# A graph attention kernel on one core: a third staged group of weights, and the order of ScalarE's first steps

## What is computed

```python
def _L0(h, adj, a):                      # slope 0.01, values h
    src = h @ a1; dst = h @ a2
    e = src[:, None] + dst[None, :]
    e = where(e > 0, e, 0.01 * e)
    e = where(adj > 0, e, NEG_INF)
    return softmax(e, axis=1) @ h
def _L1(h, adj, W, a):                   # slope 0.2, values Wh, elu behind
    Wh = h @ W
    e = leaky_relu((Wh @ a1)[:, None] + (Wh @ a2)[None, :], 0.2)
    return elu(softmax(where(adj > 0, e, NEG_INF), axis=1) @ Wh)
x = _layernorm(x + _L0(x, adj, L0_gnn_a))
x = _layernorm(x + _L1(x, adj, L1_gnn_W, L1_gnn_a))
```

## Time and profile before

| | |
|---|---|
| median of 3 runs | 438.73 us (438.42 to 439.5) |
| the profiled execution | 442.47 us, its span 440.6 us |
| busy: PE, VectorE, ScalarE, POOL | 408.1, 382.2, 382.9, 254.4 us |
| chain of work that ended last | PE 74%, VectorE 12%, issue 5%, DMA 5% |
| mean granted TensorE clock | 0.988 |

### The profile page before, as it was taken

One profiled execution on the slowest core, in us unless ns is written; L12 is line 12 of the kernel. 1 busy time (PEld: TensorE's weight loads), 2 busy tenths in 40 slices (PEclk: granted clock), 3 DMA queues, 4 the chain that ended last, 5 costly groups with the idle time before them and its releaser, 6 DMA issues.

```text
span 440.6 us, 11844 instructions
## 1 busy us (share of the span) xinstructions
PE 408.1 (93%) x4484; PEld 399.5 (91%) x4484; DVE 382.2 (87%) x682; ACT 382.9 (87%) x590; POOL 254.4 (58%) x293
## 2 busy tenths in 40 slices
PE   1599999999999999999999998999999999999980
PEld 1488889999999999999998898999999999999980
DVE  3789898899898998999889988679999999999963
ACT  3879796988969799779998989999999999999930
POOL 5523174572756637388294125659696969696831
PEclk9999999999999999999999999999999999999995
DMA  5999889989998999979510000000000000000000
GB/s 115 96 107 104 74 72 90 87 77 87 84 95 72 90 85 77 98 63 95 56 75 13 2 25 2 1 25 1 27 1 25 0 25 0 24 1 26 1 25 16
DMA packets 22766, 22.48 MB, mean 51 GB/s; under 512 B 1344, under 2 KB 22464, under 8 KB 22720
## 3 DMA queue, kind: packets, MB, share of 16 engines
q0 software_dynamic: 17424, 16.78, 44.3%
q1 hardware_dynamic: 4208, 4.05, 2.8%
q10 hardware_dynamic: 1088, 1.05, 0.7%
HBM read 69.30 MB, written 2.10 MB: 162 GB/s over the span
## 4 chain that ended last, share of the span: by engine, by line
PE 74%; DVE 12%; issue 5%; DMA 5%; POOL 1%; ACT 1%; DVEq 0%; POOLq 0%
PE acc L1222 66%; PE tb L1146 5%; DMA enc<-in_adj 3%; DVE neg L831 3%; DVE pos L842 2%; DMA mask_t<-in_x 1%; PE srcb L1156 1%; DVE mask_t L757 1%; DVE mask_t L814 1%; DVE split L814 1%; DVE wmov L820 1%; DVE scr L857 1%; ACT neg L670 1%; PE pg L1190 1%; DVE enc L814 1%
## 5 line engine op out<-in xcount | busy, mean ns | idle before, releaser
L1222 PE MATMUL acc<-wmov,pos 128*128 128x195 bf16 x2016 | 358.8, 249 | 5.0 <-DVE pos L842 3.8
L670 ACT ACTIVATE neg<-srcb,dcol 128x512 int8<-128x512 f32 x512 | 357.9, 988 | 3.4 <-PE acc L1222 3.2
L1222 PE MATMUL acc<-wmov,neg 128*128 128x195 bf16 x2016 | 358.9, 249 | 0.0
L1222 PEld LDWEIGHTS acc<-wmov,pos 128*128 128x128 fp8e4 x2016 | 199.1, 99 | 9.1 <-DVE pos L842 7.1
L1222 PEld LDWEIGHTS acc<-wmov,neg 128*128 128x128 fp8e4 x2016 | 198.1, 98 | 2.4 <-issue 1.3
L842 DVE TENSOR_TENSOR pos<-neg,mask_t 128x1024 uint16<-128x1024 uint16 x128 | 103.5, 809 | 14.1 <-PE acc L1222 0.9
L831 DVE TENSOR_TENSOR neg<-neg,mask_t 128x1024 uint16<-128x1024 uint16 x128 | 103.7, 811 | 11.6 <-ACT neg L670 9.1
L490 POOL DMA_DIRECT2D enc<-in_adj x31 | 24.7, 799 | 66.3 <-PE tb L1146 33.8
L757 DVE TENSOR_SCALAR mask_t<-tb 128x512 uint32<-128x512 uint32 (+1 forms) x64 | 43.9, 686 | 8.2 <-PE tb L1146 7.4
L1146 PE MATMUL tb<-ident,enc 128*128 128x128 f32 x256 | 39.8, 279 | 3.8 <-DMA enc<-in_adj 3.8
L742 DVE SCALAR_TENSOR_TENSOR odd<-mask_t,odd 128x1024 uint32<-128x1024 uint32 x32 | 38.8, 1212 | 0.0
(11 more groups left out here) (138 smaller groups left out, 297.8 us busy)
## 6 DMA issues: line engine op xcount, KB each, us to landing
enc<-in_adj POOLq DMA_DIRECT2D x31, 512.0 KB, 8.7
mask_t<-in_x ACTq DMA_DIRECT2D x4, 256.0 KB, 6.1
x_rows<-xout SPq DMA_DIRECT2D x8, 128.0 KB, 3.2
resid<-x_rows SPq DMA_DIRECT2D x8, 128.0 KB, 2.1
out<-xout SPq DMA_DIRECT2D x8, 128.0 KB, 1.7
wmov<-mask_t SPq DMA_DIRECT2D x2, 390.0 KB, 3.6
enc<-in_adj POOLq DMA_DIRECT2D x2, 256.0 KB, 8.7
resid<-in_a SPq DMA_DIRECT2D x1, 64.0 KB, 4.6
```

What stands on the lines that cost most here:

```text
L670: ins = nc.scalar.activation(neg[:, k % SR, :, b], srcb[:, q % 2, :], ACT.Sign, bias=dcol[:, layer, c:c + 1])
L1222: ins = nc.tensor.matmul(acc[t][:, side * WC:(side + 1) * WC], m[:, t * P:(t + 1) * P, b], wmov[:, c, side * WC:(side + 1) * WC], start=fi ...
```

## The change

Group 2 of layer 1's weights is staged as well (STAGED = 3): it is multiplied, weighed and copied in supertile 6 instead of 7, groups 1 and 2 one step earlier or in steps 5 to 7, and the groups behind it follow each a place sooner on POOL and ScalarE. On POOL, in supertile 7, group 4 is multiplied at k = 3, and groups 3 and 5 at k = 5. ScalarE's copies: groups 0, 1, 2 in supertile 6 at k = 5, 6, 7 (before: 0 and 1 at k = 6, 7), groups 3 and 4 in supertile 7 at k = 6, 7 (before 2 and 3), group 5 in step 0 of layer 1 (before groups 4 and 5 in steps 0 and 1). SP copies three groups. At the start ScalarE computes one exponential of a column of ones into `warm`, which nothing reads, before it waits for x, and the comparison of step 1 is placed ahead of the exponentials of d.

```diff
--- before.py
+++ after.py
@@ -29,7 +29,7 @@
 NOT_BINARY = 0xC7C7C7C7
 EPI = (13, 17)
 EARLY = 5
-STAGED = 2
+STAGED = 3
 LOOKS = (4, 5, 6)
 LATE_LOOKS = (2, 4, 5, 6)
 LATE = 12
@@ -99,6 +99,7 @@
         gst = sb("gst", [2, 4], F32)
         lim = sb("lim", [P, 2, 2], F32)
         strange = sb("strange", [P, 1], F32)
+        warm = sb("warm", [P, 1], F32)
         ok = sb("ok", [P, 2], F32)
         cmax = sb("cmax", [P, 2, 2], F32)
         meanv = sb("meanv", [P, F], F32)
@@ -527,9 +528,9 @@
 
                 groups = {}
                 if layer == 0 and is_last_but_one(q):
-                    groups = {3: (0,), 5: (1,)}
+                    groups = {3: (0,), 4: (1,), 5: (2,)}
                 if layer == 0 and is_last(q):
-                    groups = {3: (2,), 5: (3, 4, 5)}
+                    groups = {3: (4,), 5: (3, 5)}
                 for k in range(KB):
                     for u in loads.get(k, ()):
                         load_adj(q + 1, u)
@@ -589,6 +590,8 @@
                 act.dma_start(x_chunks[:, h * piece:(h + 1) * piece].rearrange("p (k b) d -> p k (b d)", b=NB), x_v[h])\
                     .then_inc(x_landed[h], 16)
 
+            act.wait_ge(ones_set, 1)
+            nc.scalar.activation(warm[:, :], ones[:, :], ACT.Exp)
             act.wait_ge(x_landed[0], 16)
             act.wait_ge(x_landed[1], 16)
             nc.scalar.copy(val[:, 0:half, 0:F], x_chunks[:, 0:half]).then_inc(val_set, 1)
@@ -679,9 +682,11 @@
                         copy_turned(NQ - 1)
                         group_values(NQ - 1)
                         exps_of_d(1, NB * (NQ - 1), NB * NQ, 4)
-                    compare(layer, q, k)
+                    if not (layer == 0 and is_first(q) and k == 1):
+                        compare(layer, q, k)
                     if layer == 0 and is_first(q):
                         if k == 0:
+                            compare(layer, q, 1)
                             exps_of_d(0, 0, KB * NB, 0)
                         else:
                             keep_parts(0, k - 1)
@@ -695,20 +700,20 @@
                     if layer == 0 and is_last_but_one(q):
                         if k == 3:
                             exps_of_d(1, 0, NB * EARLY, 1)
-                        if k == 6:
-                            keep_parts(1, 0)
+                        if k in (5, 6):
+                            keep_parts(1, k - 5)
                     if layer == 0 and is_last(q):
                         if k == 4:
                             exps_of_d(1, NB * EARLY, NB * (EARLY + 1), 2)
                         if k == 6:
-                            keep_parts(1, 2)
+                            keep_parts(1, 3)
                     if layer == 1 and is_first(q):
                         if k == 0:
                             group_values(NQ - 2)
                         if k == 2:
                             exps_of_d(1, NB * (NQ - 2), NB * (NQ - 1), 3)
-                        if k in (0, 1, 6):
-                            keep_parts(1, {0: 4, 1: 5, 6: 6}[k])
+                        if k in (0, 6):
+                            keep_parts(1, {0: 5, 6: 6}[k])
                     if layer == 1 and is_second(q) and k == 1:
                         exps_of_s(1, 0, NQ)
 
@@ -717,7 +722,7 @@
                     if layer == 0 and done is not None and k == KB - 1:
                         copy_turned(done[1])
                         if is_last(q) or is_last_but_one(q):
-                            keep_parts(1, 3 if is_last(q) else 1)
+                            keep_parts(1, 4 if is_last(q) else 2)
                     if done is not None and done[0] == 1 and k == 5:
                         elu(done[1])
 
@@ -748,7 +753,7 @@
                 if is_last(q):
                     if k == 0:
 
-                        dve.wait_ge(w_act, NQ + STAGED)
+                        dve.wait_ge(w_act, NQ + 2)
                     for g in range(STAGED):
 
                         if k == steps_of(g)[0]:
@@ -1059,8 +1064,8 @@
                         if k == 2:
                             take_max(1)
                             centre(1, 0, NB * EARLY)
-                        if k in (4, 6):
-                            weigh(1, k // 2 - 2)
+                        if k in (4, 5, 6):
+                            weigh(1, k - 4)
 
             def finish():
```

## The result

The change is slower: 441.93 us median of 14 runs (441.39 to 443.26) against 438.81 us (438.42 to 441.8). The ratio is 1.0056, interval [1.0042, 1.0070]: +2.5 us [1.8, 3.1]. The forecast was +1.3 us, just inside "within 0.3%"; the case that came is "slower by over 0.3%", the measured change is about twice the forecast one, and the median of the changed kernel lies 0.6 us above the end of the wide range (441.3).

The account below looks back on a forecast made before the run. PE was taken as the bound, with ScalarE right behind in layer 1. Start +0.2 and boundary +1.1 gave +1.3 us on the 438.73 us median: 440.0 us, own range 439.1 to 440.9.

Parts of the forecast that it names:

- the wide range: Whole kernel: 437.1 to 441.3 us, taking in most of the fast rival and the slow one.
- the start: First steps of layer 0: POOL's first product 1.07 us later, mostly covered by VectorE's waits for PE; +0.2 us.
- the staged part: Supertile 6 through the layer boundary: ScalarE's late copies, ending with the last turned rows, delay PE; +1.1 us.
- clearly slower rival: Start: not covered, POOL's products stretch VectorE instructions; 1.07 in place of 0.2 us, 440.9 us; chance 0.15.
- The clock: Start: PE's matmuls might reach the higher clock level sooner; only the 0.2 us could go, 439.8 us.
- The exponential: Start: table load's 1.28 us leave ScalarE's path, but the first comparison starts only 0.25 us sooner.
- Supertile 6: Supertile 6 into 7: VectorE waits 1.1 us for POOL, comparison of 7.0 starts at 212.1, PE gap 0.8 us.
- The Trainium skill's rule against it: VectorE's first subtraction beside POOL's xout: full blocking would cost up to 0.6 us, giving 440.6 instead of 440.0.
- The staged copies: Supertile 7, SP's three moves: first lands in about 4.3 us, VectorE idles 1.4 us, costing nearly nothing.
- The boundary: Supertile 7 into layer 1: removed 1.71 us used up waiting for POOL; late ScalarE copies cost +1.1 us.
- faster rival: Boundary: 1.71 us leave VectorE's chain if signs of 7.0 stand before about 213.5; -1.5, 437.2 us; chance 0.27.
- The signs to look for: Right: PE gap about 0.8 us at 216. Wrong: signs of 7.0 before 213.5, boundary PE idle under 3 us.

Follow-up runs that it names:

- e4: Kernel before with only the second comparison moved ahead of the exponentials of d; ratio 1.0022, +1.0 us.
- e2: Kernel before with both start edits, early exponential and moved comparison, and two staged groups; ratio 1.0019, +0.8 us.
- e3: Kernel before with only the early exponential of a column of ones added; ratio 0.9998, -0.1 us.
- e1: The change without its two start edits, so only the staged part, timed against the kernel before; ratio 1.0044, +1.9 us.
- e6: Against the kernel before: three staged groups, groups 0 and 1 in before's order, group 2 behind in step 7, later copies as in the change; 1.0035, +1.5 us.
- e5: Kernel before, two staged groups, with only the change's order in supertile 6; ratio 1.0044, +1.9 us.
- e10: As e9, but supertile 6 as before and group 2 made in supertile 7, staged; against the kernel before ratio 1.0019, +0.8 us.
- e7: The change's staged part with before's start and ScalarE's copies of groups 3 to 5 in before's places; against the kernel before 1.0020, +0.9 us.
- e9: e6 with ScalarE's copies of groups 3 to 5 in before's places, as in e7; against the kernel before ratio 1.0011, +0.5 us.
- e8: Kernel before with eight more identity transposes on PE between its first two turned blocks; ratio 0.9992, -0.4 us.
- e12: e10 with two staged groups, group 2 going straight to its place; against the kernel before ratio 0.9994, -0.3 us.
- e11: e4 with the comparisons of step 0.2 also ahead of the exponentials of d; against the kernel before ratio 1.0090, +3.9 us.

## Why the prediction was right and wrong

The direction was right and the size about half: +1.3 forecast, +2.5 [1.8, 3.1] measured. Two terms of the sum were too small, the start (0.2, measured 1.0) and the staged part (1.1, measured 1.9). Both errors go the same way and nothing cancelled; the direction was no luck, but the sum was no close hit either.

- **The start: the step that failed.** Forecast +0.2, measured +1.0 [0.4, 1.4] (e4) for the comparison and 0.8 [0.4, 1.3] for both edits (e2). That POOL's product is about 1.07 us later was right in mechanism (0.87 against before's trace, 1.24 against e3's; the times in the working, 16.35 and 15.26, give 1.09). That 0.16 and 0.70 us of VectorE's waits cover it was wrong. The wait of 0.70 is there only where PE's matmuls become short late (0.61 us in e1, 0.25 in e6, none in the rest), and the one of 0.16 only in before's profiled execution. The start of the transposes, 23.07, which I took as fixed, varies too: in e3 they start at 22.31 and in the changed kernel at 22.75.
- **The clearly slower rival.** The price of the start is that of this rival (1.07), its reason wasn't: POOL's products stretch VectorE's subtractions in the changed kernel by no more than 0.3 us over e3 (1.59 against 1.30 at the most). The cover is absent. The sign named for it, VectorE more than 0.2 us late at its copy of 29.04, didn't come (29.10) though its price did, since before's trace had waits and a late product of its own.
- **The clock.** The remark that an earlier rise changes at most 0.2 us was wrong: before's execution is 2.83 us behind e3's by the block of 0.5, about 2.5 without its late first product, and 1.65 of that are two stretched subtractions, which the earlier trace rows leave out.
- **The exponential: right.** The table load left ScalarE's path and brought nothing: -0.1 us [-0.6, +0.4] (e3).
- **Supertile 6: right in mechanism, mis-sized.** VectorE's wait was forecast at 1.1 and measured 0.94, the comparison of 7.0 at 212.1, measured 211.20, which is 212.5 with the 1.3 us that this trace is early against before's; ScalarE's waits are where they were forecast. But the term "two subtractions of group 1 in 1.4 us" measured 2.5, since xout and group 2's product run beside them. So the gap came one step earlier, at 6.6, with 1.03 us, and PE had lost 1.23 us by the block turned in 6.7 and 1.88 by the one in 7.1, where the forecast had 0.8 in all.
- **The Trainium skill's rule against it.** I took 0.75 us for the first subtraction; it took 1.10 beside an xout of 0.61. By the rule of the Trainium skill (SBUF — State Buffer, on the shared port pair) it would have been up to 0.6 longer than 0.75. The second, of 0.70, took 1.45: it began at 206.13, and POOL's product (205.51 + 1.52) ended at 207.03; a block to there and 0.70 behind it gives 207.73, measured was 207.58. In e5, which has no product of group 2 there, the first took 1.10 as well and the second 0.70. The rule was nearer than my sum both times, and I had applied it to one of three meetings.
- **The staged copies: right that they cost little, in part by luck.** They landed faster than I took (4.3 us for the first; in e10 it took 4.6), and two mask copies waited little:

```profile
DMA to landing us min/median/max: 2.6/2.6/2.9
...
222.71 0.69 DVE L762 TENSOR_SCALAR mask_t<-tb 128x512 uint32<-128x512 uint32 x1 [0.33 <-DMA wmov<-mask_t]
...
225.92 0.69 DVE L762 TENSOR_SCALAR mask_t<-tb 128x512 uint32<-128x512 uint32 x1 [0.46 <-DMA wmov<-mask_t]
```

  e10 shows the price where VectorE is in time: 2.15 us.
- **The boundary: right in mechanism, and the sum too small.** PE got 0.57 us back between 7.1 and 7.5 (1.88 to 1.31), which I had put at nothing; that the removed 1.71 us bring them isn't shown, since e5 gets the same 0.57 with nothing removed. ScalarE's wait was forecast at nearly 3 us and measured 2.67; the waits of VectorE for signs 0.34 and 0.53; the late turned rows cost 0.39 (1.61 to 2.00), where 0.5 was forecast. Altogether the staged part costs 1.9 us, forecast 1.1. The terms that were too small are the subtractions of supertile 6 (1.4, measured 2.5) and what hangs on them: the order of supertile 6 alone costs 1.9 (e5). ScalarE's early copies are worth 1.0 (e1 against e7). These two don't add to 1.9, so they overlap, and the 0.8 can't be split between them.
- **The faster rival** (1.71 us leave VectorE's chain) was half true: e7 regains 1.1 us in the boundary, 0.57 of which e5 regains too. Its condition, that the signs of 7.0 are in time, isn't what decides: in e7 VectorE starts neg of 7.0 at 212.47, which is 215.45 with the 2.98 us that this trace is early, as late as in the changed kernel (214.10 + 1.30), and it regains them all the same. What differs is where ScalarE copies groups 3 to 5.
- **The signs to look for:** the gap of about 0.8 us was forecast at 216 and lay at 208; less than 3 us of PE idle time in the boundary stretch was named as a sign against the forecast, and 3.0 came, so by that sign the matter was open; part of the loss stands ahead of that stretch.

## What to carry to other kernels

An idle time that hides an edit is worth only as much as it is there in every execution: look whether the runs of the kernel spread, and which of them the profiled one is, before an edit is costed at nothing. Work moved out of a stretch where VectorE is the bound needs a free place on *each* engine of its chain: here the third product met VectorE's subtractions in both places tried in supertile 6, and ScalarE's copy, one step sooner, made it wait 2.7 us with the next comparisons queued behind. And a staging area over data that arrive later moves a wait to the earliest step that it covers.

## What the runs showed that I had not expected

PE's matmuls of 195 columns take 0.35 to 0.37 us at first and 0.25 later; their starts are 0.163 us apart at first and 0.087 later. (A step has 32 of them, 16 pairs, as the x32 of the earlier trace rows has it, and not 32 pairs.) With nearly the same work on PE ahead of it, the rise comes at 21.2, 22.5, 22.6 or 22.8 us in some profiled executions (e9, e8, e7, e3), at 23.3 to 25.1 in others (e2, e10, e4, e5, the change), and at 26.2 to 27.5 in the rest (e12, e6, e1, e11, before). The granted clock was 1.00 in every microsecond from 8 to 40 us of the trace of before, so that row doesn't show it. The Trainium skill (TensorE: Matmul & The Clock Gate, part 1) says that the point of the rise varies from run to run, and gives plus or minus half a microsecond for it. These traces agree that it varies, but theirs are 6.3 us apart, and the measurement decides here. Why it comes when it comes isn't shown. The runs of e3 stayed within 438.5 to 439.8 us (12 runs), those of before reached 441.8; whether the early exponential does that or chance, 12 runs don't settle.
